# A layer norm, a cross attention and a second layer norm as three programs or as one

## The reference, cut to what matters

```
x = _layernorm(x + attention(x))                # window attention, then the first norm
kv  = ctx_512 @ W_k.T + b_k                     # (4, 256, 64)
out = einsum('bij,bjd->bid', x, kv)
sim = einsum('bid,bjd->bij', out, kv) * 256**-0.5
mu, var = mean(sim, -1), var(sim, -1)
sim = (sim - mu) * rsqrt(var + 1e-6) * ln_gamma + ln_beta
x = _layernorm(x + softmax(sim, -1))            # the second norm
x = _layernorm(x + routed_mixture(x))           # the next block
```

## Time and profile before

| | us |
|---|---|
| median of 3 runs | 1832.23 (1831.49 to 1837.68) |
| the profiled execution | 1848.18 |
| its span | 1846.4 |
| first norm, start to the next function's first instruction | 298.8 to 308.84 |
| cross attention, to the second norm's first instruction | 308.84 to 366.16 |
| second norm, to the router | 366.16 to 376.21 |

### The profile page before, as it was taken

The page is one execution under the profiler, slowest core; times in us unless marked ns, Lnnn a source line. Parts: engine busy times, 40 slices in busy tenths (PEclk is TensorE's granted clock), DMA queues, the critical chain, the costliest instruction groups (busy, mean ns, idle before and its releaser), DMA issues. The chain is left out here.

```text
span 1846.4 us, 25267 instructions
## 1 busy us (share of the span) xinstructions
PE 1408.2 (76%) x9198; PEld 930.8 (50%) x9198; DVE 889.8 (48%) x1982; ACT 472.4 (26%) x1093; POOL 421.9 (23%) x418
## 2 busy tenths in 40 slices
PE   5999996246815668889898975888888853899876
PEld 2865864123413336667677854344444432344465
DVE  4365363472285576666654134555555543222234
ACT  0431430111102446445443121233333321000010
POOL 2353351416510333223221011311111101000000
PEclk9999997567766889888876567999999985899988
DMA  2000002906530102121111101000000001411001
GB/s 100 18 28 11 18 11 86 270 28 170 134 146 10 44 18 38 24 36 19 26 22 17 16 17 46 20 21 20 21 20 21 1 1 52 175 36 41 17 23 45
DMA packets 155187, 86.32 MB, mean 47 GB/s; under 512 B 91097, under 2 KB 149184, under 8 KB 154448
## 3 DMA queue, kind: packets, MB, share of 16 engines
q1 hardware_dynamic: 151152, 71.66, 14.9%
q0 software_dynamic: 3936, 13.34, 2.0%
HBM read 70.52 MB, written 16.32 MB: 47 GB/s over the span
## 5 line engine op out<-in xcount | busy, mean ns | idle before, releaser
L2336 PE MATMUL fp_acc<-fp_xe,fp_w 128*128 128x512 f32 x384 | 167.4, 599 | 17.8 <-DMA fp_w<-in_L_ffn_v_proj 17.8
L1490 DVE SCALAR_TENSOR_TENSOR dh_acc<-dh_pj,dh_conv,dh_acc 128x510 f32<-128x510 f32 x144 | 107.3, 746 | 94.3 <-ACT dh_acc L1373 90.8
L2336 PEld LDWEIGHTS fp_acc<-fp_xe,fp_w 128*128 128x128 f32 x384 | 73.8, 192 | 111.1 <-issue 92.3
L2157 POOL TENSOR_TENSOR la_qrot<-la_prod 128x512 f32<-128x512 f32 x48 | 60.5, 1275 | 280.5 <-DVE la_prod L2077 217.8
L1186 PE MATMUL dh_pj<-xT,dh_w 128*128 128x512 f32 x192 | 104.8, 675 | 7.1 <-DMA dh_w<-in_L_attn_Wq 6.2
L2313 DVE TENSOR_TENSOR fp_xe<-xT,fa_wb 128x2048 f32<-128x2048 f32 x16 | 36.6, 2292 | 129.7 <-PE fp_acc L2336 119.0
L2010 ACT ACTIVATE la_e<-la_sc,la_nmax 128x256 f32<-128x256 f32 x128 | 59.0, 473 | 145.3 <-DVE la_nmax L2086 145.3
L1856 PE MATMUL la_qb<-xT,la_wabs 128*128 128x512 f32 x192 | 91.7, 604 | 1.0 <-ACT la_mabs L1994 1.0
L217 POOL MEMSET n_half<- 128x8 f32 x6 | 0.6, 105 | 392.3 <-POOLq L131 360.4
L180 PE MATMUL n_tp<-const,x 128*128 128x128 f32 x80 | 22.9, 446 | 82.4 <-DVE x L208 82.3
L395 POOL TENSOR_TENSOR wa_qkT<-wa_t_cos,wa_t_sin 128x512 f32<-128x512 f32 x40 | 50.9, 1273 | 124.4 <-DVE wa_t_sin L371 124.4
(11 more groups left out here) (410 smaller groups left out, 3105.9 us busy)
## 6 DMA issues: line engine op xcount, KB each, us to landing
placed<-mw_rows SPq DMA_DIRECT2D x8, 768.0 KB, 8.1
mw_gu<-in_L_ffn_w_gate SPq DMA_DIRECT2D x16, 384.0 KB
mw_gu<-in_L_ffn_w_up SPq DMA_DIRECT2D x16, 384.0 KB
mw_d<-in_L_ffn_w_down SPq DMA_DIRECT2D x16, 384.0 KB
mw_rows<-placed SPq DMA_DIRECT2D x8, 768.0 KB, 6.9
fa_wb<-w_table POOLq DMA_DIRECT2D x3, 2048.0 KB, 18.1
const<-in_const SPq DMA_DIRECT2D x1, 2176.5 KB, 10.6
wa_wq<-in_L_attn_q_kernel SPq DMA_DIRECT2D x4, 512.0 KB, 3.8
```

The costliest lines, as they stand in the source:

```text
L1490: dve.scalar_tensor_tensor(dst, src[:, :, 0:SEQ - j], conv[:, a, m, D_CONV - 1 - j:D_CONV - j], dst, ALU.mult, ALU.add).then_inc(tapped, 1)
L2157: pool.tensor_tensor(qrot[:, c, n, :], prod[:, c, 2 * n, :], prod[:, c, 2 * n + 1, :], ALU.add).then_inc(rotated, 1)
L2336: mm = pe.matmul(acc[:, m, c, :], w_s[:, s, m, k, :], xe[:, s, k, 512 * c:512 * c + 512], start=first and k == 0, stop=last and k == KC - 1)
```

## The change

The three functions become one, `cross_with_norms`, with one barrier at its end in place of three. Three loads that the keys need have a semaphore of their own (`kv_loaded`), and PE computes and transposes the keys ahead of the tiles' transposes; ACT, not DVE, evicts them. All eight tiles' similarities are held in four PSUM banks (`sim(t)`). Their statistics are taken for four tiles at a time, with the factor 256**-0.5 folded into the epsilon, and the power of four tiles is one POOL instruction (`root`). ACT centres a tile (`center`, with `shift` = -mean x rstd), two buffers become four (`RING`), and the second norm's statistics are taken inside the softmax loop, each three turns behind. POOL computes `root(2, 0)` between tiles 6 and 7. ACT issues the two stores to `x_rows` after its last copy. `normalize` loses its `ew` branch; its other calls stay. The diff, cut (semaphores and small tensors are left out, and the lines of `softmax_cross`, which are printed above):

```diff
-            if ew is not None:
-                @block.sync
-                def _(sp):
-                    view = ew.x_rows.rearrange("(t p) c -> p t c", p=P)
-                    for n in range(2):
-                        sp.wait_ge(tile_ready, 4 * n + 4)
-                        sp.dma_start(view[:, 4 * n:4 * n + 4, :], env.x[:, 4 * n:4 * n + 4, :]).then_inc(ew.kept, 16)
...
-def softmax_cross(nc, env, ew, ctxT, wkT, bk, gamma, beta):
+def cross_with_norms(nc, env, ew, ctxT, wkT, bk, gamma, beta):
+    SCALE, EPS, H = float(DIM) ** -0.5, 1e-6, TILES // 2
+    RING = 4
...
+        n1, n2, n3, e = sb("n1", [P, RING, DIM]), sb("n2", [P, RING, DIM]), sb("n3", [P, RING, DIM]), sb("e", [P, RING, DIM])
+        kp, kt, tp = ps("kp", [P, 2, 512]), ps("kt", [P, 2, 512]), ps("tp", [P, 4, 512])
...
+        sim = lambda t: tp[:, t // 2, DIM * (t % 2):DIM * (t % 2) + DIM]
...
+                sp.dma_start(ctx_sb[:], ctxT).then_inc(kv_loaded, 16)
+                sp.dma_start(w_sb[:], wkT).then_inc(kv_loaded, 16)
+                sp.dma_start(b_sb[:], bk.rearrange("(d o) -> d o", o=1)).then_inc(kv_loaded, 16)
+                sp.dma_start(g_sb[:], gamma.rearrange("(o d) -> o d", o=1).to_broadcast([P, DIM])).then_inc(affine_loaded, 16)
+                sp.dma_start(be_sb[:], beta.rearrange("(o d) -> o d", o=1).to_broadcast([P, DIM])).then_inc(affine_loaded, 16)
                 ew.prefetch(sp)
...
+                pe.wait_ge(kv_loaded, 48)
                 for c in range(2):
+                    pe.matmul(kp[0:CTX, c, :], w_sb[:], ctx_sb[:, 512 * c:512 * c + 512], start=True, stop=True).then_inc(kv_done, 1)
                 pe.wait_ge(biased, 2)
                 for t in range(TILES):
+                    mm = pe.transpose(kt[:, 0, CTX * t:CTX * t + CTX], kvT[:, P * t:P * t + P], env.c("ident")[0:CTX, 0:CTX])
+                mm.then_inc(kv_turned, 1)
+                def turn(ready, bank, done_sem, th, kc):
+                    for j in range(4):
+                        t = 4 * th + j
+                        pe.wait_ge(ready, t + 1)
+                        mm = pe.transpose(bank[:, P * j:P * j + P], env.x[:, t, P * kc:P * kc + P], env.c("ident"))
+                    mm.then_inc(done_sem, 1)
+                def attend(c):
+                    pe.wait_ge(copied[c], 2)
+                    for b in range(2 * c, 2 * c + 2):
+                        for k in range(KC):
+                            mm = pe.matmul(kp[0:CTX, c, SEQ * (b % 2):SEQ * (b % 2) + SEQ], kv[:, 2 * b + k, :], env.xT[:, k, SEQ * b:SEQ * b + SEQ], start=(k == 0), stop=(k == KC - 1))
+                    mm.then_inc(o_done, 1)
+                def similar(c):
+                    pe.wait_ge(o_copied, c + 1)
+                    pe.wait_ge(copied[0], 2)
+                    pe.wait_ge(copied[1], 2)
+                    for t in range(H * c, H * c + H):
+                        b = t // 2
+                        mm = pe.matmul(sim(t), oT[:, P * t:P * t + P], kvT[:, SEQ * b:SEQ * b + SEQ], start=True, stop=True)
+                        if t % 2:
+                            mm.then_inc(sim_done, 1)
+                for th in range(2):
+                    for kc in range(KC):
+                        turn(tile_ready, tp[:, 2 * th + kc, :], turned, th, kc)
                 pe.wait_ge(kv_copied, 1)
+                attend(0)
+                attend(1)
+                similar(0)
+                similar(1)
+                for th in range(2):
+                    for kc in range(KC):
+                        turn(tile2_ready, (kp, kt)[th][:, kc, :], turned2, th, kc)
+            @block.scalar
+            def _(act):
+                act.wait_ge(kv_loaded, 48)
+                for c in range(2):
+                    act.wait_ge(kv_done, c + 1)
+                    act.activation(kvT[:, 512 * c:512 * c + 512], kp[0:CTX, c, :], ACT.Identity, bias=b_sb[:, 0:1]).then_inc(biased, 1)
+                act.wait_ge(kv_turned, 1)
+                act.copy(kv[:], kt[:, 0, :].rearrange("p (t d) -> p t d", d=CTX)).then_inc(kv_copied, 1)
+                for th in range(2):
+                    act.wait_ge(turned, 2 * th + 2)
+                    act.copy(env.xT[:, 1, 512 * th:512 * th + 512], tp[:, 2 * th + 1, :]).then_inc(copied[th], 1)
+                def center(t):
+                    act.wait_ge(shift_done, t // H + 1)
+                    if t >= RING:
+                        act.wait_ge(scaled, t - RING + 1)
+                    act.activation(n1[:, t % RING, :], sim(t), ACT.Identity, bias=shift[:, t:t + 1], scale=rstd[1][:, t:t + 1]).then_inc(centered, 1)
+                def power(t):
+                    act.wait_ge(max_done, t + 1)
+                    if t >= RING:
+                        act.wait_ge(added, t - RING + 1)
+                    act.activation(e[:, t % RING, :], n3[:, t % RING, :], ACT.Exp, bias=mx[:, t:t + 1], accum_out=total[:, t:t + 1]).then_inc(exp_done, 1)
+                for i in range(TILES + 3):
+                    if i < TILES:
+                        center(i)
+                    if i >= 3:
+                        power(i - 3)
+                act.wait_ge(o_done, 2)
+                for th in range(2):
+                    act.wait_ge(turned2, 2 * th + 2)
+                    act.copy(env.xT[:, 1, 512 * th:512 * th + 512], (kp, kt)[th][:, 1, :]).then_inc(copied2, 1)
+                view = ew.x_rows.rearrange("(t p) c -> p t c", p=P)
+                for n in range(2):
+                    act.wait_ge(tile2_ready, H * n + H)
+                    act.dma_start(view[:, H * n:H * n + H, :], env.x[:, H * n:H * n + H, :]).then_inc(ew.kept, 16)
             @block.vector
             def _(dve):
+                def statistics(j, t, src):
+                    dve.bn_stats(stats[j][:, t, :], src).then_inc(stats_done[j], 1)
+                def moments(j, c, eps):
+                    for t in range(H * c, H * c + H):
+                        dve.wait_ge(stats_done[j], t + 1)
+                        dve.bn_aggr(mv[j][:, t, :], stats[j][:, t, :]).then_inc(aggr_done[j], 1)
+                    dve.wait_ge(aggr_done[j], H * c + H)
+                    dve.tensor_scalar(var[j][:, H * c:H * c + H], mv[j][:, H * c:H * c + H, 1], eps, None, ALU.add).then_inc(var_done[j], 1)
+                def scale(j, t, ready):
+                    if t % H == 0:
+                        dve.wait_ge(rstd_done[j], t // H + 1)
+                    dve.tensor_scalar(env.x[:, t, :], env.x[:, t, :], mv[j][:, t, 0:1], rstd[j][:, t:t + 1], ALU.subtract, ALU.mult).then_inc(ready, 1)
                 for c in range(2):
+                    for t in range(H * c, H * c + H):
+                        statistics(0, t, env.x[:, t, :])
+                    moments(0, c, LN_EPS)
+                for t in range(TILES):
+                    scale(0, t, tile_ready)
+                for th in range(2):
+                    dve.wait_ge(turned, 2 * th + 1)
+                    dve.tensor_copy(env.xT[:, 0, 512 * th:512 * th + 512], tp[:, 2 * th, :]).then_inc(copied[th], 1)
                 for c in range(2):
+                    dve.wait_ge(o_done, c + 1)
+                    dve.tensor_copy(oT[:, 512 * c:512 * c + 512], kp[0:CTX, c, :]).then_inc(o_copied, 1)
+                for c in range(2):
+                    for t in range(H * c, H * c + H):
+                        dve.wait_ge(sim_done, t // 2 + 1)
+                        statistics(1, t, sim(t))
+                    moments(1, c, EPS / (SCALE * SCALE))
+                for c in range(2):
+                    dve.wait_ge(rstd_done[1], c + 1)
+                    dve.scalar_tensor_tensor(shift[:, H * c:H * c + H], mv[1][:, H * c:H * c + H, 0], -1.0, rstd[1][:, H * c:H * c + H], ALU.mult, ALU.mult).then_inc(shift_done, 1)
+                def largest(t):
                     dve.wait_ge(shifted, t + 1)
+                    dve.tensor_reduce(mx[:, t:t + 1], n3[:, t % RING, :], AX, ALU.max, negate=True).then_inc(max_done, 1)
+                def finish(t):
                     dve.wait_ge(exp_done, t + 1)
                     dve.reciprocal(rec[:, t:t + 1], total[:, t:t + 1]).then_inc(rec_done, 1)
                     dve.wait_ge(rec_done, t + 1)
+                    dve.scalar_tensor_tensor(env.x[:, t, :], e[:, t % RING, :], rec[:, t:t + 1], env.x[:, t, :], ALU.mult, ALU.add).then_inc(added, 1)
+                for i in range(TILES + 3):
                     if i < TILES:
+                        largest(i)
+                    if 2 <= i < TILES + 2:
+                        finish(i - 2)
+                    if i >= 3:
+                        dve.wait_ge(added, i - 2)
+                        statistics(2, i - 3, env.x[:, i - 3, :])
+                    if i == H + 2:
+                        moments(2, 0, LN_EPS)
+                moments(2, 1, LN_EPS)
+                for t in range(H):
+                    scale(2, t, tile2_ready)
+                dve.wait_ge(o_done, 2)
+                dve.wait_ge(turned2, 1)
```

(78 more changed lines are left out.)

46 lines of the change are left out of this document (4 added, 42 removed).

## The result

The changed kernel takes 1814.9 us (median of 4 runs, 1811.08 to 1817.84) against 1832.35 us for the kernel before (4 runs, 1831.49 to 1837.68): 17.5 us less by the medians. The ratio on record is 0.9888, with a 95% interval of 0.987 to 0.9906; of 1832.35 us that is 20.5 us less, 17 to 24. The forecast was 1812.2 with a range of 1806 to 1821.

A forecast was written before the change was run, and what follows sets the result against it. SP's prefetch issuing (56.2 us) was taken as the bound, the work ending 2.8 us earlier; starting it 10.04 us sooner puts the router at 356.15, not 376.2, so 1832.2 - 20.0 = 1812.2 us, range 1806 to 1821.

The forecast's parts named there:

- SP's limit: Fused function: SP's prefetch issuing, 56.2 us, sets the end; router no sooner than 356.15, gain 20.05 us; chance 0.48.
- Keys and products: Fused function's head: keys, then `attend` halves of 3.3 and 1.7 us; POOL's first product at 324.3, 331.08 before.
- The loop: Softmax tiles: POOL sets the pace, 1.48 us a tile plus 0.48 standing still beside DVE's add, 1.96 for tiles 3 to 6.
- Tail and stores: Behind tile 7: second norm's statistics 4.5 us, scaling to copies 5.7 plus about 0.5, ACT's two stores 0.37 each.
- rival A: Fused function's end: the work, not SP, ends last, needing over 2.8 us more; 1814.8 to 1818.1 us; chance 0.33.
- The sum of the work: Fused function: all work and its barrier end at 353.3, 2.8 us before SP's limit.
- The cover: Fused function's end: the 2.8 us by which the work ends before SP's limit.
- rival A's three conditions: Clock low through `attend(1)` and `similar`, 3.6 us; DVE's add waiting, up to 2.9; stores 1.7 to 2.3 more.
- the page's rule: SBUF lock goes to whoever starts first; DVE's add would also wait, up to 0.72 us a tile, 2.9 over four.
- A's second condition: Tile loop: DVE's add waits for POOL's product, up to 4 x 0.72 = 2.9 us.
- B: Tile loop keeps 3.87 us a tile, for example through ACT table loads; gain 10.5 or 8.5 us; chance 0.07.
- the routed experts gain nothing and lose nothing: Behind the fused function: gather needs `x_rows` tens of us later; clearing and weights land as early before use as before.

The follow-up runs named there:

- fused_sp_late: Changed kernel, but SP waits for the first norm's transposed tiles before beginning the prefetch; ratio to the kernel before 0.996.
- three_fast_loop: Kernel before, three functions kept, cross attention replaced by the changed kernel's middle without the fusing with the norms; ratio to the kernel before 0.9993.
- fused_short_late_root: Changed kernel, last two of eight weight groups issued at the routed experts' start and `root(2, 0)` moved behind tile 7; ratio to the kernel before 0.987.
- fused_short_prefetch: Changed kernel, with the last two of eight expert weight groups issued at the start of the routed experts; ratio to the kernel before 0.9855.
- three_again: The kernel before, unchanged, run once more on the third chip; ratio 1.0006.
- three_short_prefetch: Kernel before, three functions, with the last two of eight expert weight groups issued at the routed experts' start; ratio to the kernel before 1.0001.
- fused_third: The changed kernel word for word, run again on the third chip; ratio to the kernel before 0.9891.

## Why the prediction was right, and by how much its terms were off

**SP's limit (right).** The forecast had the router at 57.35 us from the fused start (356.15 - 298.8), set by SP at 56.2. Measured were 56.0, 59.0 and 57.2 with SP at 54.9, 57.9 and 56.1. `fused_sp_late` and `three_fast_loop` show the cause from both sides: later issuing with the same work lengthens the part, and shorter work with the same issuing doesn't shorten it. The gain is that the prefetch starts a norm and a barrier sooner (10.0 us) and that the second norm and its barrier lie beside it (10.1 us). On the third chip it is 77.1 - 57.2 = 19.9 us.

**Keys and products (right, the clock a little better).** PE's first product began 3.94 us after the start (forecast 4.1). The granted clock was 0.50 at 311.0 to 314.5 and 1.00 at 316 to 317, so the rise fell early in `attend(0)` and both halves took 4.16 us (forecast 3.3 + 1.7). POOL's first product came 23.2 us after the start (forecast 25.5).

**The loop (mechanism right, size off).** The term of 0.48 a tile for POOL standing still beside DVE's add was mis-sized; POOL lost 0.15: 1.63 a tile and not 1.96, 1.3 us over four tiles. The stop for `root(2, 0)` was 1.94 + 1.02 = 2.96 (forecast 3.1). `fused_short_late_root` took 2.4 us out of the part by moving it.

**Tail and stores (right).** From tile 7's maximum to the scaling 3.9 us (forecast 4.5), from there to the last copy 6.0 (6.2). The two stores took 1.00 us to issue together against 0.74, while SP's load beside them took 1.43 and its last three 1.1 to 2.3 each. So the high end that rival A needed was not there: ACT's stores didn't take as long as SP's loads. The prediction took that high end from the earlier trace rows, which shows one of two kinds of load from L573; the other reached 3.63 us.

**The sum of the work.** 54.5 us were forecast up to where it would open the barrier; by the trace it is 349.61 + 1.00 + 0.73 - 301.53 = 49.8, and 50.1 where it really opened it (`fused_short_prefetch`). The cover was 6 us and not 2.8, so the other engines stood idle before the barrier for 7 us and not for 1 to 3. This error of 4.7 us lies on the side that doesn't show in the time, which is luck: the same error the other way would have made the work the end. None of rival A's three conditions came true (where the prediction speaks of the page's rule, it calls A's second condition the second rival): the clock rose early in the first of the two products, DVE's add took 0.48 throughout, and the stores took 1.00 together. B is refuted: no table load stands between ACT's centring and exponentials.

**The step that failed: "the routed experts gain nothing and lose nothing".** They lose 0.7 to 2.9 us up to the gather in these traces: 41.5 to 42.5 us in the changed kernel's three traces against 39.6 and 40.8. The first piece is the router's products. In the first trace of the kernel before and in `three_again` the granted clock rose at the very end of the second norm's transposes and stood at 1.00 when the router began. In `three_short_prefetch` and `three_fast_loop` the same transposes, in one block of the same length, ended at 0.50, and the scores came at 7.1 us. The windows of `three_again`:

```profile
373.00:374.50 1.50, 0.95 (x5) 0.55 (x3) 0.69 (x1) 0.51 (x1) 0.00 (x0) 0.71 0.85 298
375.40:377.00 1.60, 1.60 (x15) 1.60 (x16) 0.53 (x3) 1.19 (x1) 0.66 (x3) 1.00 0.06 10
```

and those of `three_fast_loop`:

```profile
372.00:374.20 2.20, 1.51 (x8) 1.10 (x6) 0.69 (x1) 1.01 (x2) 0.00 (x0) 0.50 0.83 284
374.90:376.50 1.60, 1.60 (x8) 1.60 (x8) 0.52 (x3) 1.24 (x1) 0.70 (x3) 0.50 0.04 10
```

In all eight traces of fused kernels without filling products the scores came at 7.1 us too. There the transposes are split by DVE's copy, and PE then stood idle for 2 to 20 us. So the high clock was had in two of four traces of three functions and in none of eight fused ones. That the splitting is the cause is only argued, and two traces had the low clock without it. The low clock costs 1.8 to 2.0 us.

The second piece is a collision, in the changed kernel:

```profile
371.66 0.69 DVE L907 TENSOR_TENSOR me_cand<-me_scb,me_gm 128x512 f32<-128x512 f32 x1
371.69 3.45 POOL L1005 TENSOR_TENSOR me_s_u<-me_s_h,me_s_u 96x512 f32<-96x512 f32 x2 [13.40 <-ACT me_s_u L844]
372.39 1.64 DVE L908 TENSOR_TENSOR me_cand<-me_cand,me_gpen 128x512 f32<-128x512 f32 x1
```

DVE's product (L908) took 1.64 us instead of 0.69, and POOL's had already begun. By the page "SBUF — State Buffer" of the Trainium skill (section "SBUF: two separate sides") a DVE operation with two inputs in SBUF and a POOL operation that reads SBUF share a pair of ports, and whichever starts first holds it to its end while the other waits. This row agrees. No row of the first trace showed DVE held. The changed kernel shows it once more, at the head of its tile loop, where POOL's first product began at 324.78 and lasted 0.73:

```profile
324.85 0.68 DVE L578 SCALAR_TENSOR_TENSOR xc_shift<-xc_mv,xc_rstd 128x4 f32<-128x4 f32 x1 [1.06 <-POOL xc_rstd L615]
```

The same operation for the first four tiles took 0.16. In the loop POOL's second product agrees only in part: 0.28 us of DVE's add were left when it began, and it took 0.15 longer.

The collision of L908 isn't the change's own: `three_again` has 1.75 at the same place, `fused_third` 0.69. On the third chip 0.7 us of the 19.9 are lost by the gather (40.8 against 41.5), and the medians there differ by 17.2; the interval of the ratio of 0.9891 is 14 to 26 us.

**What stays open.** From the third norm on the four traces of the third chip differ by several us either way (1295.9 to 1302.5; 1298.4 and 1300.3 for `three_again` and `fused_third`), which one trace each can't tell from nothing. So the time, 2.7 us from the forecast, can't confirm the smaller terms of the sum.

## What to carry to other kernels

Before shortening a chain inside a block, ask which engine opens the barrier behind it: an engine that only issues transfers counts, and here it made a loop that was twice as fast worth nothing until its issuing could begin earlier and more work could lie beside it. When programs are fused over such a limit, write down both lengths, the issuing's and the work's, and the gap between them, as the gap says what further work on either is worth. Filling TensorE's idle time before the router gave it the high clock, but in both kernels that did so the filling itself then held the barrier for as long. A filling that ends before whatever else opens the barrier was not run.

## What the runs showed of the hardware

- POOL and DVE held each other both ways: POOL's product of 128 x 256 took 0.87 instead of 0.72 us where DVE's two-input add was still running when it began, and DVE's product of 128 x 512 took 1.64 to 1.75 instead of 0.69 us where POOL's had begun first.
- ACT issued two stores of 512 KB in 1.00 us together at a DMA share of about 1.1, while single loads of 384 KB from SP took 1.1 to 2.3 us to issue. In `fused_short_late_root` SP's first load after a pause of 2.5 us took 0.37 us to issue, though the DMA share in the pause was 1.12.
- The same 24 loads and 8 stores, with SP's ten small loads, kept SP for 54.9 to 57.9 us in the changed kernel, in three traces with the same order of issues.
- From the gather to the third norm it took 115 to 120 us in nine traces and 131 to 135 in five. The three groups had 114.9 to 120.3, 131.4 to 133.0 and 115.0 to 116.6 us, fused or not; why the second differs is not shown.
